# A transformer layer on one core: the setup rebuilt, with tables first, the maximum and the vector product on TensorE, and the first two heads projected straight into the stacked layout

## The reference, cut to what matters

```python
w_emb = fake_quant(emb_weight)                 # scale = max|w| / 127; round(w / scale) * scale
x = pad(w_emb[tokens], one step in front)
h = relu(depthwise_conv(x, fake_quant(conv_weight)))          # context of 2 tokens

def _sn_weight(W, u, sigma):
    v = W @ u;    v = v / norm(v)
    u2 = W.T @ v; u2 = u2 / norm(u2)
    return W / (v @ W @ u2) * sigma
qkv = layernorm(h) @ _sn_weight(w_qkv, u_qkv, sigma_qkv).T
dots = q @ k.T * exp(temperature); diagonal = -max; attn = softmax(dots)
h = h + (attn @ v) @ _sn_weight(w_out, u_out, sigma_out).T + b_out
h = h + mixture_ffn(layernorm(h))              # groups of 16 tokens, 16 x 4 experts
```

## Time and profile before

| | us |
|---|---|
| median of 3 runs (lowest, highest) | 539.45 (538.0, 540.36) |
| the profiled execution | 537.22 |
| its span | 535.5 |

### The profile page before, as it was taken

The page is one execution under the profiler, slowest core; times in us unless marked ns, Lnnn a source line. Parts: engine busy times, 40 slices in busy tenths (PEclk is TensorE's granted clock), DMA queues, the critical chain, the costliest instruction groups (busy, mean ns, idle before and its releaser), DMA issues.

```text
span 535.5 us, 10598 instructions
## 1 busy us (share of the span) xinstructions
PE 488.9 (91%) x3562; PEld 400.1 (75%) x3562; DVE 408.5 (76%) x738; ACT 375.7 (70%) x682; POOL 243.1 (45%) x236
## 2 busy tenths in 40 slices
PE   0378799999999999999999999999999999988678
PEld 0363578888888888778788888888888888873454
DVE  0368398987888788788887787788778999889452
ACT  0115388888788878887888788878877886827675
POOL 1222167376635663754246645654673455532000
PEclk9959899999999999999999999999999999998969
DMA  7404902932592178243522692087209520000002
GB/s 236 183 1 99 226 1 52 205 72 80 104 197 73 31 155 168 79 90 66 122 66 65 125 196 81 15 171 144 78 16 195 115 80 1 0 1 1 2 11 70
DMA packets 32766, 49.13 MB, mean 92 GB/s; under 512 B 3419, under 2 KB 23637, under 8 KB 32469
## 3 DMA queue, kind: packets, MB, share of 16 engines
q1 hardware_dynamic: 32004, 47.75, 38.6%
q10 hardware_dynamic: 720, 0.85, 0.6%
HBM read 6.65 MB, written 1.05 MB: 14 GB/s over the span
## 4 chain that ended last, share of the span: by engine, by line
PE 82%; DVE 5%; issue 4%; ACT 4%; DMA 3%; POOL 1%; SPq 1%; DVEq 0%; POOLq 0%; ACTq 0%
PE ps L653 22%; PE ps L639 21%; PE ps L623 11%; PE ps L624 11%; PE ps L588 4%; PE ps L692 3%; PE ps L824 2%; ACT v_all L970 2%; PE ps L627 2%; DMA conv_sb<-in_conv 2%; ACT v_all L992 1%; PE ps L583 1%; PE ps L835 1%; DMA q_st<-arena 1%; SPq L474 1%
## 5 line engine op out<-in xcount | busy, mean ns | idle before, releaser
L420 POOL TENSOR_SCALAR probs<-probs,inv_sum 128x1024 f32<-128x1024 f32 x128 | 144.8, 1131 | 196.4 <-DVE inv_sum L1208 196.3
L1214 DVE TENSOR_REDUCE neg_max<-ps 128x1 f32<-128x1024 f32 x128 | 156.7, 1224 | 73.5 <-PE ps L627 73.3
L932 ACT ACTIVATE pt_hi<-ps 128x512 fp32r<-128x512 f32 x256 | 139.2, 595 | 40.5 <-PE ps L639 40.4
L1202 DVE TENSOR_TENSOR pt_lo<-ps,pt_hi 128x512 fp32r<-128x512 f32 x256 | 162.5, 676 | 1.5 <-ACT pt_hi L932 1.5
L653 PE MATMUL ps<-pt_hi,v_slot 128*128 128x256 f32 x512 | 149.7, 325 | 0.0
L952 ACT ACTIVATE probs<-ps,neg_max 128x1024 f32<-128x1024 f32 x128 | 142.5, 1113 | 1.1 <-ACT x2t L916 0.3
L639 PE MATMUL ps<-ident,probs 128*128 128x128 f32 x1024 | 133.5, 273 | 0.0
L653 PE MATMUL ps<-pt_lo,v_slot 128*128 128x256 f32 x512 | 127.8, 281 | 0.0
L639 PEld LDWEIGHTS ps<-ident,probs 128*128 128x128 f32 x1024 | 110.1, 141 | 0.3
L623 PE MATMUL ps<-k_hi,q_st 128*128 128x512 f32 x256 | 101.7, 397 | 5.4 <-DMA q_st<-arena 4.3
L653 PEld LDWEIGHTS ps<-pt_hi,v_slot 128*128 128x128 f32 x512 | 96.5, 189 | 9.2 <-issue 9.2
(11 more groups left out here) (132 smaller groups left out, 444.6 us busy)
## 6 DMA issues: line engine op xcount, KB each, us to landing
k_hi<-arena SPq DMA_DIRECT2D x32, 256.0 KB, 4.8
k_lo<-arena SPq DMA_DIRECT2D x32, 256.0 KB, 5.1
q_st<-arena SPq DMA_DIRECT2D x32, 256.0 KB, 3.7
v_slot<-v_all SPq DMA_DIRECT2D x16, 512.0 KB, 4.6
arena<-arena SPq DMA_DIRECT2D x28, 256.0 KB, 4.8
f_sb<-in_f SPq DMA_DIRECT2D x2, 1024.0 KB, 10.4
w_slot<-in_w_pairs SPq DMA_DIRECT2D x9, 128.0 KB, 2.1
x<-in_tok SPq DMA_DIRECT2D x2, 512.0 KB, 11.6
```

The lines of the kernel that those rows point to most:

```text
L420: pool.tensor_scalar(probs[:, t % 4, :], probs[:, t % 4, :], inv_sum[:, t % 4:t % 4 + 1], 1.0, ALU.mult, ALU.mult).then_inc(norm_done, 1)
L932: act.activation(dst, ps[:, transposes_bank(t, a, drain), :].rearrange("p (j c) -> p j c", c=P), ACT.Copy).then_inc(hi_done, 1)
L1202: dve.tensor_tensor(pt_lo[at], ps[:, transposes_bank(t, a, drain), :].rearrange("p (j c) -> p j c", c=P), pt_hi[at].bitcast(F32), ALU.subt ...
L1214: dve.tensor_reduce(neg_max[:, t % 4:t % 4 + 1], ps[:, SCORES + 2 * (t % 2):SCORES + 2 * (t % 2) + 2, :].rearrange("p a c -> p (a c)"), AX ...
```

## The change

- DVE starts with the embedding's maxima per row, spreads them on a diagonal, and PE multiplies with ones, so that every partition holds all 125 and DVE takes the maximum there; POOL's all-reduce is gone.
- v is computed by PE: 12 matmuls of the transposed weights (`wt_sb`, `wv_sb`) with u as one column, and 4 with `wo_sb`. They stand in PE's list ahead of the embedding. POOL's products and DVE's sums are gone. wr and wor (the row form, for u2) are loaded once the first tokens have landed.
- The first two heads' q and k are projected with weights that hold each head twice (`w_twice`), so that the result is already stacked; ACT and DVE write high and low straight into `q_st`, `k_hi`, `k_lo`. Head 0 is done in the setup, head 1 in steps (0,4) to (0,7). The projections for pair 1 move to (1,1) to (1,4).
- The eight value projections move from the setup into steps (0,0) to (0,3), two in each; heads 0 and 1 go straight into `v_slot`.
- `add_bias(0)` moves from the setup into step (1,5); the second batch's one-hot rows are made after head 0's q and k.

```diff
@@ -247,14 +255,14 @@
             return sorted(work)
 
         def highs(work):
...
-        SETUP_QK = {"k0": WORK, "k1": 0, "q0": 1, "q1": 2}
+        FIRST_HEAD = {"dk0": WORK, "dk1": TRANS, "dq0": 2, "dq1": TRANS + 1}
+        FIRST_VALUES = [PV_BANK, TRANS, TRANS + 1, PV_BANK, TRANS, TRANS + 1, PV_BANK, WORK]
...
-            pool.wait_ge(setup_dve, 3)
-            pool.partition_all_reduce(qs[:, 1:2], qs[:, 0:1], P, MAX_OVER_PARTITIONS).then_inc(setup_pool, 1)
-
-            pool.wait_ge(wqkv_loaded, 32)
-            pool.tensor_tensor(wu_sb, wr_sb, u_row.unsqueeze(1).broadcast_to([P, 12, D]), ALU.mult
-                               ).then_inc(setup_pool, 1)
-            pool.wait_ge(wout_loaded, 16 * 5)
-            pool.tensor_tensor(wou_sb, wor_sb, uo_row, ALU.mult).then_inc(setup_pool, 1)
...
-            pool.wait_ge(attn_loaded, 64)
-            add_bias(0)
...
+                        if (k, t) == (1, 5) and pair.i == 0:
+                            pool.wait_ge(attn_loaded, 32)
+                            add_bias(0)
...
-            sp.dma_start(uo_row, u_out.partition_broadcast(P)).then_inc(wout_loaded, 16)
-            sp.dma_start(wor_sb, wo_rows).then_inc(wout_loaded, 16)
-            weights(0)
-            sp.dma_start(wv_sb[:, :], wv).then_inc(attn_loaded, 16)
+            tokens(0)
+            sp.dma_start(u_sb[:, :], u_cols).then_inc(wt_loaded, 16)
+            sp.dma_start(wt_sb.rearrange("p i w c -> p i (w c)"), w_pairs[0:H // 2].rearrange("i d c -> d i c")
+                         ).then_inc(wt_loaded, 16)
+            sp.dma_start(wv_sb[:, :], wv).then_inc(proj_loaded, 16)
+            sp.dma_start(wo_sb[:, :, :], wo_pairs).then_inc(proj_loaded, 16)
+            sp.dma_start(twice_sb.rearrange("p w k c -> p (w k c)"), w_twice).then_inc(twice_loaded, 16)
+            tokens(1)
+            weights(1)
             sp.dma_start(b_sb[:, :], b_out.partition_broadcast(P)).then_inc(attn_loaded, 16)
-            sp.dma_start(wo_sb[:, :, :], wo_pairs).then_inc(attn_loaded, 16)
             sp.dma_start(wo_last[:, :, :], wo_twice).then_inc(attn_loaded, 16)
...
-            sp.wait_ge(work_read, 2)
-            head_part(0, 1)
-            sp.wait_ge(work_read, 4)
-            head_part(0, 0)
-            weights(1)
-            sp.wait_ge(v_lo_done, NT)
-            head_v(0, 0)
...
+            pe.wait_ge(const_ready, N_CONST)
+            pe.wait_ge(setup_dve, SETUP_DIAG)
+            pe.matmul(top, ones[0:VOCAB, :], quant[0:VOCAB, 0:VOCAB], start=True, stop=True).then_inc(setup_pe, 1)
+
+
+            pe.wait_ge(wt_loaded, 32)
+            for t in range(12):
+                if t == 8:
+                    pe.wait_ge(proj_loaded, 32)
+                rows = wt_sb[:, t % 4, t // 4, :] if t < 8 else wv_sb[:, (t - 8) * P:(t - 7) * P]
+                pe.matmul(v_ps[:, t:t + 1], rows, u_sb[:, 0:1], start=True, stop=True)
+            for j in range(H // 2):
+                last = pe.matmul(v_ps[:, 12:13], wo_sb[:, j, :], u_sb[:, 1 + j:2 + j], start=j == 0,
+                                 stop=j == H // 2 - 1)
+            last.then_inc(setup_pe, 1)
+
             pe.wait_ge(setup_dve, SETUP_TABLES)
             pe.wait_ge(one_hot_ready, 2)
             embed(0).then_inc(h_mm, 1)
             embed(1).then_inc(h_mm, 1)
 
-            pe.wait_ge(setup_dve, SETUP_VECTORS)
+
+            pe.wait_ge(rows_loaded, 32)
+            pe.wait_ge(setup_act, 2)
             for t in range(12):
-                last = pe.matmul(ps[:, 6, 0:1], wr_sb[:, t, :], norm_sb[:, t:t + 1],
-                                 start=t == 0, stop=t == 11)
-            last.then_inc(setup_pe, 1)
+                pe.matmul(u2_ps[:, 0:1], wr_sb[:, t, :], norm_sb[:, t:t + 1], start=t == 0, stop=t == 11)
             for t in range(4):
-                last = pe.matmul(ps[:, 7, t:t + 1], wor_sb[:, t * P:(t + 1) * P], norm_sb[:, 12:13],
+                last = pe.matmul(u2_ps[:, 1 + t:2 + t], wor_sb[:, t * P:(t + 1) * P], norm_sb[:, 12:13],
                                  start=True, stop=True)
             last.then_inc(setup_pe, 1)
...
+            def project_twice(kind, k, bank):
+
+                which, c = "qk".index(kind[1]), int(kind[2])
+                return pe.matmul(ps[:, bank, :], twice_sb[:, which, k, :], xt[:, c * HALF:(c + 1) * HALF], start=True, stop=True)
+
+            pe.wait_ge(twice_loaded, 16)
+            for kind, bank in FIRST_HEAD.items():
+                pe.wait_ge(xt_done, int(kind[2]) + 1)
+                project_twice(kind, 0, bank).then_inc(first_mm, 1)
+                if kind == "dk0":
 
                     pe.wait_ge(setup_dve, SETUP_SQUARES)
-                    pe.matmul(ps[:, 4, 0:4], ones[:, :], norm_sb[:, 18:22], start=True, stop=True
+                    pe.matmul(square_ps, ones[:, :], norm_sb[:, 18:22], start=True, stop=True
                               ).then_inc(setup_pe, 1)
-            pe.wait_ge(attn_loaded, 64)
-            pe.wait_ge(setup_dve, SETUP_RATIO)
-            for t in range(NT):
-                if t == 3:
-                    pe.wait_ge(work_read, 1)
-                if t >= 4:
-                    pe.wait_ge(v_lo_done, t - 3)
-                project_values(t, 4 + t % 4).then_inc(v_mm, 1)
-            pe.wait_ge(work_read, 4)
+
+            def first_values(t):
+
+                for i in (2 * t, 2 * t + 1):
+                    if i == 2:
+                        pe.wait_ge(first_lo, 4)
+                    if i >= 3:
+                        pe.wait_ge(v_lo_done, 2 * min(i - 2, 4))
+                    if i == 7:
+                        pe.wait_ge(work_read, 2)
+                    project_values(i, FIRST_VALUES[i]).then_inc(v_mm, 1)
...
-                if t == 0:
+                if pair.i == 0:
+                    if k == 0 and t == 0:
+                        pe.wait_ge(first_lo, 3)
+                    if k == 1 and t in (0, 4):
+                        pe.wait_ge(work_read, pair.use_of("dq1" if t else "dq0"))
+                elif t == 0:
                     pe.wait_ge(qk_loaded[k], 6 * pair.slot_loads)
...
+                    if begins:
+                        pe.wait_ge(v_lo_done, 2 * NT)
+                    if c_local == 0 and not direct:
                         pe.wait_ge(vs_loaded[slot], slot_loads)
...
-                    pe.wait_ge(v_lo_done, NT)
+                    pe.wait_ge(v_lo_done, 12)
...
+                if fresh and t < 4:
+                    first_values(t)
...
                     ins = project_qk(kind)
+                elif kind[0] == "d":
+                    pe.wait_ge(v_lo_done, 2 * NT)
+                    ins = project_twice(kind, 1, WORK)
...
-            act.dma_start(u_row, u_qkv.partition_broadcast(P)).then_inc(wqkv_loaded, 16)
-            act.dma_start(wr_sb, wqkv_rows).then_inc(wqkv_loaded, 16)
             for i, x in enumerate((sigma_qkv, sigma_out, temperature)):
-                act.dma_start(sig[:, i:i + 1], x.partition_broadcast(P)).then_inc(wout_loaded, 16)
+                act.dma_start(sig[:, i:i + 1], x.partition_broadcast(P)).then_inc(sig_loaded, 16)
+            act.wait_ge(tok_loaded[0], 16)
+            act.dma_start(wr_sb, wqkv_rows).then_inc(rows_loaded, 16)
+            act.dma_start(wor_sb, wo_rows).then_inc(rows_loaded, 16)
...
+            act.wait_ge(setup_pe, 2)
+            act.activation(norm_sb[:, 0:13], v_ps, ACT.Copy).then_inc(setup_act, 1)
             embedded(0)
             embedded(1)
...
+            act.wait_ge(setup_pe, 3)
+            act.activation(norm_sb[:, 13:18], u2_ps, ACT.Copy).then_inc(setup_act, 1)
...
+            def high_twice(kind, k, bank):
+
+                half = slice(int(kind[2]) * HALF, (int(kind[2]) + 1) * HALF)
+                if kind[1] == "q":
+                    return act.activation(q_st[:, k, half], ps[:, bank, :], ACT.Copy, scale=q_scale)
+                return act.activation(k_hi[:, k, half], ps[:, bank, :], ACT.Copy)
...
+                high_twice(kind, 0, bank).then_inc(first_hi, 1)
+
+            def first_values(t):
+
+                for i in (2 * t, 2 * t + 1):
+                    act.wait_ge(v_mm, i + 1)
+                    bank = ps[:, FIRST_VALUES[i], :].rearrange("p (h c) -> p h c", c=DH)
+                    act.activation(v_slot[:, 0:2, i, 0:DH], bank[:, 0:2, :], ACT.Copy, scale=v_scale
+                                   ).then_inc(v_hi_done, 1)
+                    act.activation(v_all[:, i, 2:H, 0:DH], bank[:, 2:H, :], ACT.Copy, scale=v_scale
+                                   ).then_inc(v_hi_done, 1)
...
+                        first = pair.i == 0 and k == 0 and t < 4
+                        if first:
+                            first_values(t)
+                            exponentials(pair, k, t)
                         work(pair, k, t)
                         output(pair, k, t)
-                        exponentials(pair, k, t)
+                        if not first:
+                            exponentials(pair, k, t)
...
```

(53 more changed lines are left out.)

162 lines of the change are left out of this document (68 added, 94 removed).

## The result

After the change the kernel takes 533.74 us (median of 6 runs, 532.34 to 536.59), before it 537.92 us (6 runs, 536.96 to 540.36): ratio 0.9923, 95% interval 0.9896 to 0.9950. That is 2.7 to 5.6 us shorter, clear of the noise but under 1%; predicted were 534.0 us and -5.3 us. The profiled execution of after took 536.59 us (span 534.9) and is the slowest of its six; the same code in a later set took 533.27 us in its profiled execution (span 531.5, 534.64 us median of 8, ratio 0.9923, 0.9895 to 0.9950).

The account below looks back on a forecast made before the run. It took a setup chain of latencies as the bound before step 16, and TensorE from there to 477 us. Terms -20.6 + 9.7 + 3.7 + 1.9 = -5.3 us gave a 534.0 us median; own range 531 to 537, with rivals 528 to 540.

Parts of the forecast that it names:

- Gain before the scores: Setup up to the first scores: they start at 35.4 us instead of 56.0, a gain of 20.6 us.
- Part 1: Tables in the setup: without the all-reduce DVE's chain is 2.4 us shorter; tables and one-hot rows stand at 12.9 us.
- Part 2: v on TensorE, queued before the embedding: 32 instructions, 7.0 us; v ends and the embedding starts at 18.5 us.
- Part 3: Embedding to first q/k projection: x_hat complete at 29.0 us, u2 done at 27.2, projection at 29.0 instead of 38.52.
- Part 4: Scales and direct layout: scores can start 6.4 us after the first projection's start, at 35.4 us.
- S: Start of the first q/k projection in the setup: predicted at 29.0 us, before the change 38.52.
- The loop: First sixteen attention steps, with twelve added projections: 58.4 us against 48.7, a loss of 9.7 us.
- The wait: Step 16 waits 3.7 us for head 2's q/k transfers, because k1 moves from step 9 to step 12.
- The clock behind it: PE at a lowered clock after idling before step 16: costs 1.9 us, half of 3.75.
- Rival A: Step 16's stall or its clock price is absent: 528.5 to 532 us, chance 0.27.
- Rival B: ACT and DVE hold the first nine steps longer, or u2 runs at half clock: 537 to 538 us, chance 0.18.
- Rival C: Rows wr and wor land late, at 26 us, delaying u2 in the setup: 540.4 us, chance 0.10.

Follow-up runs that it names:

- second trace: The unchanged code of the changed kernel, profiled again in a later set: 534.64 us median, ratio 0.9923 to the kernel before.
- allreduce_back: Changed kernel with POOL's all-reduce again in place of the diagonal, PE's product and the maximum: 533.58 us, ratio 0.9916 to the kernel before.
- embed_between: Changed kernel with PE's embedding between v's first half and the half needing wv and wo: 533.28 us, ratio 0.9912 to the kernel before.
- best: Changed kernel with k1 at step 10 and the embedding between v's halves together: 527.10 us, ratio 0.9791 to the kernel before.
- bias_back: Changed kernel with add_bias(0) back on POOL in the setup: 535.21 us, ratio 0.9951 to the kernel before.
- k1_step11: Changed kernel with the four projections for pair 1 one step earlier, in steps 8 to 11: 527.89 us, ratio 0.9804 to the kernel before.
- k1_step10: Changed kernel with pair 1's q0 in step 2 and q1, k0, k1 in steps 8 to 10: 526.74 us, ratio 0.9771; in another set 527.40 us, 0.9798.
- keep_warm: Changed kernel with five unread value projections on PE behind step 15, during the wait: 530.84 us, ratio 0.9850 to the kernel before.

## Why the prediction was right

**How close, and how much of it is luck.** 533.74 us against 534.0 looks closer than it is. The forecast set out from 539.45, the median of three runs; six runs put it at 537.92, 1.5 us lower. The gain was 4.2 us and not 5.3. The two errors nearly cancel.

**Gain before the scores: -20.6 predicted, -20.1 measured** (56.01 to 35.94; -21.1 in the second trace). The terms are less good than their sum:
- Part 1: the convolution table came at 7.75, not 6.2 (the scaling by bytes was too kind; 9.86 before), and stood at 14.2, not 12.9. It did not matter, by allreduce_back: the embedding waits for v.
- Part 2: that v holds up the embedding in PE's queue is right (embed_between). The wait inside v was wrong: wv and wo were taken to land at 15.0, and landed 5.6 and 6.6 us after their issues (4.63 and 5.18), at 10.2 and 11.8. PE went from wt's matmuls into theirs without a gap. v ran for 32 x 0.22 us from wt's landing on (10.44, predicted 10.1), and the embedding started at 17.33, not 18.5. The 0.22 us were taken from rows at the half clock without a word on why v should run at it; it did. Behind the embedding, with the pace doubled, 8 such matmuls took 0.95 us (best, 20.82), so the 7 us of v are what these instructions cost at the half clock only.
- Part 3: u2 was to end at 27.2 at the full clock, with the half clock as the other end (30.7). It ended at 28.0 and did both: most of it fast, the rest slow. In the second trace it ended at 27.1, all at the full clock. The step that failed in the first trace is "the embedding leaves the clock up": it does so for 2 to 5 us, and 4 were needed. From then on PE, not x_hat (28.22, predicted 29.0), sets the first projection: 29.75 against 29.0.
- Part 4: it took 6.2 us from S to the scores, predicted 6.4, and the 2.24 us of the product were POOL's doing (bias_back).

**The loop: +9.7 predicted, +9.1 measured** (57.8 for sixteen steps against 48.7). Step 4 came at +16.3 (predicted +16.5), step 8 at +31.5 (+31.9). The walk over ACT and DVE was sound.

**The wait: 3.7 predicted, 4.29 measured**, 4.2 to 4.4 in the six traces that have k1 at step 12 and nothing for PE to do in the gap. The chain k1, split, six issues, landing took 13.6 us, against 12.7 to 13.7, and the transfer landed at +62.0 from the first scores (predicted +62.1). PE was there at +57.8 instead of +58.4: that is the excess. k1_step11 and k1_step10 show that the place of k1 is the cause.

**The clock behind it: 1.9 predicted.** Step 16 took 5.62 us in the profiled execution (2.8 too many), 4.5 to 5.2 in five others with the wait (1.6 to 2.4 too many). keep_warm shows that idling is the cause. The 1.9 us lie inside that range, and the profiled execution lies above them.

**Sum.** -20.1 + 9.1 + 4.3 + 2.8 = -3.9, and step 17 moved by -3.9 (-5.9 in the second trace); predicted -5.3 in all. The median moved by -4.2. The profiled execution itself was only 0.6 us shorter than that of before: from step 17 to the end it took 431.25 us, before 427.96. What differs there is the time at the half clock: over 440 to 526 us the mean granted clock is 0.88 in after and 0.92 in before. One trace of a changed kernel, bias_back, has 0.94 there and needs 427.7 us, as little as before, so the change does not force the longer end. But the ten others need 429.8 to 431.25, and before has only one trace; whether the change makes the low clock there more frequent is open. Rival A (no stall, no clock price) did not occur: both are there in every trace of this code. Its wv and wo that land at 11 did occur (10.2 and 11.8), and did not put S at 27: v's 7 us from 10.44 on, and not the loads, then set the embedding's start. Rival B (the first nine steps slower) fell with the loop's +9.1; its other half, u2 at the half clock, came in part and cost 1.2 us in the first trace. Rival C (rows landing at 26) fell: u2 started right behind the embedding, at 23.2.

## What to carry to other kernels

When work is moved later in a loop to shorten a setup, follow what hangs on its last piece to the next stage that needs it, and count the slack in steps: here k1 moved by three steps, the transfers behind it take 13.6 us, and the stall with its clock price cost 5.9 to 7.1 of the 20 us gained; one step back gave 2.9 us of the wait at once. Shortening one chain (the tables) is worth nothing while another (v) stands in front of it in the same engine's queue; read the queue order before pricing the edit. And a wait of TensorE can have two prices, its length and the clock afterwards: 4.2 to 4.4 us of idling brought the second here, 1.42 us did not. When new matmuls are priced, look at the clock under which the rows they are priced from ran: u2's one-column matmuls took 0.22 us at one level and 0.12 at the other.

## What was unexpected in the hardware

- The granted clock of TensorE fell to 0.50 in the setup while PE was busy, 2 to 5 us after the embedding, for 3.4 to 10.4 us. Before the change the same level lay over 29.38 to 38.50. What PE had been doing before the fall was u2's one-column matmuls, in two traces with v's second half ahead of them and in some the transposes behind them; whether they are the cause no run tests. The moment differs between executions of one program: u2's last 8 matmuls took 1.84 us in one trace of after and 1.03 in the other.
- The same happens at the end: over 440 to 526 us the mean granted clock is 0.88 in after and 0.90 in its second trace. The first needs 1.4 us more than the second from step 17 to the end, and 2.0 us more up to it: single traces of this kernel cannot settle 1 us.
- A granted clock of 1.00 at the start of a profile can mean that there is no record. The embedding's matmuls went from 0.43 us a pair to 0.22 at 21.9 us (chain of waits above), while the table of stages prints 1.00 for all of 17.33:23.20. The first record of the clock in that trace begins at 21.99 us; for the time before it the view prints 1.00. In all twelve traces, that of before included, the pace of the embedding doubles within 0.1 us of the first record, 3.0 to 6.1 us after the embedding's start. So up to there PE ran at the pace of the half clock, in v's one-column matmuls too, and these, 3.6 to 7 us of them, had not raised it.
- A 2-column product on DVE takes 14 times as long (2.24 against 0.16 us) when a 128x1024 addition on POOL starts 0.12 us before it. That the addition makes the difference is shown; in what way it holds up the product is not.
- POOL's all-reduce starts at the same moment of the span in two kernels (13.64 and 13.57 us), 3.03 and 5.2 us after its operand is there.
